# A fused attention and ternary feed-forward kernel: GpSimd adds twelve of the sixteen key chunks in every block, and the work around the row maxima is put in another order

## What is computed

```python
q = (x @ Wq.T + bq).reshape(Bx, Lx, H, hd)      # k_ and v the same way
scores = jnp.einsum('bqhd,bkhd->bhqk', q, k_) * scale + bias[None, None, None, :]
attn = jax.nn.softmax(scores, axis=-1)
ctx = jnp.einsum('bhqk,bkhd->bqhd', attn, v).reshape(Bx, Lx, Dx)
y = x + ctx @ Wo.T + bo                         # then layer norm with gamma, beta
x = _layernorm(x + attention)
x = _layernorm(x + ffn(x))                      # ffn: x @ Hadamard, 4 bit rounding, ternary weights
```

## Time and profile before

| what | value |
|---|---|
| median of 3 runs | 4854.95 us (4854.8 to 4855.31) |
| the profiled execution | 4854.98 us, its span 4853.2 us |
| TensorE busy | 4667.6 us, 96% |
| VectorE busy | 3318.9 us, 68% |
| ScalarE busy | 2596.1 us, 53% |
| GpSimd busy | 3642.9 us, 75% |

### The profile page before, as it was taken

How to read it: one execution, slowest core, us unless ns; L and a number is a source line. 1 busy time by engine, 2 the same in 40 slices (tenths; PEclk the granted TensorE clock), 3 DMA queues, 4 the chain that set the end, 5 groups by cost and what they waited for, 6 DMA issues and landing times.

```text
span 4853.2 us, 83960 instructions
## 1 busy us (share of the span) xinstructions
PE 4667.6 (96%) x24152; PEld 2375.4 (49%) x24152; DVE 3318.9 (68%) x5886; ACT 2596.1 (53%) x4891; POOL 3642.9 (75%) x1215
## 2 busy tenths in 40 slices
PE   7999999999899999999989999999999999999987
PEld 4445545554544555554454454555545444554434
DVE  3776676666777666666767767666676776667637
ACT  1455555554555555555455555555545655555545
POOL 1687777887488887777748877788875888877885
PEclk8899999999999999999999999999999999999998
DMA  9113232324411333322441223333334123332112
GB/s 207 32 40 71 58 72 63 70 66 105 127 40 43 66 70 69 75 62 64 114 112 41 56 60 71 67 66 67 76 112 99 50 48 66 70 68 59 29 53 72
DMA packets 245915, 346.30 MB, mean 71 GB/s; under 512 B 14801, under 2 KB 100561, under 8 KB 245458
## 3 DMA queue, kind: packets, MB, share of 16 engines
q1 hardware_dynamic: 245458, 340.73, 29.6%
HBM read 205.33 MB, written 33.55 MB: 49 GB/s over the span
## 4 chain that ended last, share of the span: by engine, by line
PE 78%; POOL 7%; DMA 6%; issue 4%; DVE 2%; ACT 1%; SPq 1%; POOLq 0%; ACTq 0%; DVEq 0%
PE ps_m L544 25%; PE ps_s L559 19%; PE ps_o L585 15%; PE ps_z L564 5%; DMA qst<-lo 5%; PE ps_z L531 4%; PE ps_m L505 3%; PE ps_z L499 3%; POOL acc L1117 3%; POOL prob L1143 1%; POOL prob L1147 1%; PE ps_s L505 1%; POOL prob L1132 1%; PE ps_s L499 1%; POOL prob L1126 1%
## 5 line engine op out<-in xcount | busy, mean ns | idle before, releaser
L926 DVE TENSOR_REDUCE umax<-ps_m 128x1 f32<-128x512 f32 x4096 | 2497.1, 681 | 757.7 <-PE ps_m L544 757.7
L1117 POOL TENSOR_TENSOR acc<-acc,prob 128x2048 f32<-128x2048 f32 x624 | 2858.2, 4580 | 151.2 <-ACT prob L783 101.7
L783 ACT ACTIVATE prob<-ps_s 128x512 f32<-128x512 f32 x4096 | 2131.5, 609 | 940.9 <-PE ps_s L559 927.1
L544 PE MATMUL ps_m<-kst,qst 97*128 97x512 f32 x4096 | 1872.0, 460 | 57.6 <-DMA qst<-lo 36.9
L559 PE MATMUL ps_s<-qst,kst 99*128 99x512 f32 x4096 | 1635.5, 400 | 12.2 <-ACT prob L783 9.9
L544 PEld LDWEIGHTS ps_m<-kst,qst 97*128 97x128 f32 x4096 | 777.7, 190 | 996.0 <-DVE umax L926 738.0
L585 PE MATMUL ps_o<-prob,vst 128*32 128x512 f32 x8192 | 976.7, 600 | 0.0
L559 PEld LDWEIGHTS ps_s<-qst,kst 99*128 99x128 f32 x4096 | 780.2, 191 | 138.9 <-ACT prob L783 31.5
L1117 POOL TENSOR_TENSOR acc<-prob 128x2048 f32<-128x2048 f32 x64 | 291.1, 4548 | 401.2 <-ACT prob L783 401.2
L585 PEld LDWEIGHTS ps_o<-prob,vst 128*32 128x32 f32 x8192 | 228.0, 110 | 530.8 <-issue 331.1
L1101 POOL TENSOR_TENSOR obuf<-obuf,zinv 128x512 f32<-128x512 f32 x64 | 82.4, 1287 | 442.1 <-ACT obuf L810 442.1
(11 more groups left out here) (114 smaller groups left out, 2528.8 us busy)
## 6 DMA issues: line engine op xcount, KB each, us to landing
xk<-in_xT_dram SPq DMA_DIRECT2D x66, 1024.0 KB, 8.6
xq<-in_xT_dram SPq DMA_DIRECT2D x65, 1024.0 KB, 5.8
kst<-hi SPq DMA_DIRECT2D x128, 256.0 KB, 6.8
qst<-hi SPq DMA_DIRECT2D x128, 256.0 KB, 5.2
wq<-in_wT_dram SPq DMA_DIRECT2D x65, 256.0 KB, 6.1
kst<-lo SPq DMA_DIRECT2D x64, 256.0 KB, 5.6
qst<-lo SPq DMA_DIRECT2D x64, 256.0 KB, 3.9
ctxT_dram<-obuf SPq DMA_DIRECT2D x64, 256.0 KB, 2.4
```

Source lines behind the costliest of these rows:

```text
L544: nc.tensor.matmul(ps_m[:, u % NMB, :], qst[k % 2][0:RSTACK, h, qt * P:(qt + 1) * P], kst[k // NQB % 2][0:RSTACK, h, kb * QB:(kb + 1) * QB ...
L783: nc.scalar.activation(prob[:, c % NPB, h, :], ps_s[:, (i * HG * NKC + HG * c + h) % NSB, :], ACT.Exp, scale=SCALE).then_inc(ex, 1)
L926: nc.vector.tensor_reduce(umax[:, m, kb:kb + 1], ps_m[:, u % NMB, :], AX.X, ALU.max).then_inc(mred, 1)
L1117: nc.gpsimd.tensor_tensor(acc[:], a, prob[:, c % NPB], ALU.add).then_inc(padd, 1)
```

## The change

1. `pe_sums` is `[12, 13, 14, 15]` in all blocks, so GpSimd makes eleven additions in every block, in the 16 early ones instead of ten.
2. The order within a pair's feed is the string `FEED`: the last three scores come ahead of the last three units.
3. The transpose of the maxima stands ahead of the sum of chunk 15.
4. The transfer of the maxima's row is issued by ScalarE, right behind its `mrow`, after a wait for it. SP issues the low part of the queries right behind the high parts.
5. `next_stage` (loads of inputs and weights for the next head group's projection) is issued by SP in block 0 of a batch and no longer at the end of the token stage.
6. At the program's start the second head group's projection is mixed with the 64 units of the first block.

```diff
+FEED = "msmsmsmsmssmsmsm"
 def pe_sums(i):
-    return [12, 13, 14, 15] if i >= NQB else [9, 12, 13, 14, 15]
+    return [12, 13, 14, 15]
...
@@ feed @@
-                for c in (2 * p, 2 * p + 1):
-                    for h in range(HG):
-                        u = HG * c + h
+                k, u = UP * p, UP * p
+                for what in FEED:
+                    if what == "s":
+                        c, h = divmod(k, HG)
+                        score(n, i, c, h, head=i == 0 and c == 0)
+                        k += 1
+                    else:
...
                             unit(u, n + 1, i + 1, (n >> 2) + 1 if i % NQB == NQB - 1 else None)
-                        score(n, i, c, h, head=i == 0 and c == 0)
+                        u += 1
@@ attend @@
                 for c in pe_sums(i):
+                    if c == NKC - 1 and not (last and i == NBLK - 1):
+                        maxima_to_rows(n + 1)
                     if c >= LATE_SUMS:
                         chunk_sums(n, i, c)
-                if not (last and i == NBLK - 1):
-                    maxima_to_rows(n + 1)
@@ SP, each block @@
+                        if i == 0:
+                            next_stage((n >> 2) + 1, (n >> 4) & (NB - 1), 1)
...
                             queries(n + 2, i + 2)
-                        if not (last and i == NBLK - 1):
-                            maxima(n + 1, i + 1)
-                        if not (last and i >= NBLK - 2):
                             low_queries(n + 2, i + 2)
@@ ScalarE @@
-            def maxima_rows(f):
+            def maxima_rows(f, k):
                 act.wait_ge(mtr, f + 1)
                 nc.scalar.activation(mrow[:], ps_m[0:2 * HG * NQB, 1, 0:P], ACT.Copy).then_inc(mcp, 1)
+                both = qst[k % 2][RM0:RM0 + 2].rearrange("p h (q x) -> p (h q) x", x=P)
+                act.wait_ge(mcp, f + 1)
+                act.dma_start(both.bitcast(F32), mrow[:].bitcast(F32)).then_inc(q_cur, 16)
@@ TensorE, start of the program @@
+            for t in range(NQB):
+                if t > 0:
+                    pe.wait_ge(k_lo, NQB + t)
+                keys_of(1, t, ps_z[:, :])
+                for u in range(UNITS // NQB * t, UNITS // NQB * t + UNITS // NQB // 2):
+                    unit(u, 0, 0, 0)
+                if t > 0:
+                    pe.wait_ge(v_cp, NQB + t)
+                values_of(t, ps_o[:, :])
+                for u in range(UNITS // NQB * t + UNITS // NQB // 2, UNITS // NQB * (t + 1)):
+                    unit(u, 0, 0, 0)
+                if t == 1:
+                    queries(1, ps_s[:, 0, :])
```

More of the change, by code:

```diff
@@ L326, in keys @@
                     keys_quarter(stage, b, s, t)
-                next_stage(stage, b, s)
             def next_stage(stage, b, s):
@@ L350, in next_queries @@
                 load_w(wq[:], 0, (k + 1) // NQB % NG).then_inc(wq_ld, 16)
[L352 to L356, removed]
             def store_context(n, i, stage):
@@ L420, in tokens @@
                             keys_quarter(bb * NG + NG + 1, bb, NG + 1, s - KEY_STEP - 1)
-                if not last:
-                    next_stage(b * NG + NG + 1, b, NG + 1)
             sp.dma_start(rows[0:1, 8:10, :], band.rearrange("a (b n) -> a b n", b=2)).then_inc(band_ld, 16)
@@ L437, in _ @@
             keys(0, 0, 0)
+            next_stage(0, 0, 0)
             sp.wait_ge(stk_ones, 4)
@@ L446, in _ @@
             next_queries(0, 0)
-            keys(1, 0, 1)
-            queries(1, 1)
-            low_queries(1, 1)
+            for t in range(NQB):
+                keys_quarter(1, 0, 1, t)
+                if t == 1:
+                    queries(1, 1)
+                    low_queries(1, 1)
             next_queries(0, 1)
-            maxima(0, 0)
             def batch(b, last):
@@ L718, in _ @@
             queries(0, ps_m[:, 0, :])
-            keys(1, 1)
-            queries(1, ps_m[:, 0, :])
             ternary()
@@ L724, in _ @@
             pe.wait_ge(tern_c, 5)
+            pe.wait_ge(q_lo, 1)
+            pe.wait_ge(wkv_ld, 64)
+            for t in range(NQB):
+                if t > 0:
[8 more added lines that the diff above has]
+                    unit(u, 0, 0, 0)
+                if t == 1:
+                    queries(1, ps_s[:, 0, :])
+            pe.wait_ge(k_lo, 2 * NQB)
+            pe.wait_ge(v_cp, 2 * NQB)
+            maxima_to_rows(0, first=True)
             pe.wait_ge(q_lo, 2)
-            for u in range(UNITS):
-                unit(u, 0, 0, 0)
-            maxima_to_rows(0, first=True)
             def batch(b, last):
@@ L755, in values_of, with keys @@
                                      bank, ACT.Copy).then_inc(v_cp, 1)
-            def keys(stage, s, q=None):
+            def keys(stage, s, kbank, vbank, q=None):
                 for t in range(NQB):
@@ L762, in keys @@
                         act.wait_ge(k_stk[t % 2], stage * (2 * NSTK) + NSTK)
-                    keys_of(stage, s, t, ps_m[:, 0, :])
-                    values_of(stage, s, t, ps_m[:, 1, :])
+                    if t == 2 and q is not None:
+                        act.wait_ge(q_stk, (q + 1) * NSTK)
+                    keys_of(stage, s, t, kbank)
+                    values_of(stage, s, t, vbank)
+                    if t == 1 and q is not None:
+                        act.wait_ge(k_stk[0], stage * (2 * NSTK) + NSTK)
+                        queries(q, q, ps_s[:, 0, :])
             def queries(f, k, bank):
@@ L806, in attend @@
                 if not (last and i == NBLK - 1):
-                    maxima_rows(n + 1)
+                    maxima_rows(n + 1, i + 1)
                 act.wait_ge(pv, n * NKC + 2 * NKC)
@@ L864, in _ @@
             act.wait_ge(bias_ld, 16)
-            keys(0, 0)
+            keys(0, 0, ps_m[:, 0, :], ps_m[:, 1, :])
             act.wait_ge(k_stk[0], 2 * NSTK)
             queries(0, 0, ps_m[:, 0, :])
[L868 to L871, removed]
+            keys(1, 1, ps_z[:, :], ps_o[:, :], 1)
+            maxima_rows(0, 0)
             def batch(b, last):
@@ L916, in quarter, with first_quarter, maxima @@
                 low_part(lo[:, 1], hi[:, 1], 1, i // NQB + 1, ps_z[:, :]).then_inc(k_lo, 1)
-            def maxima(f, i=None, last=False):
+            def first_quarter(t):
+                if t == 0:
+                    dve.wait_ge(q_stk, NSTK)
+                dve.wait_ge(k_hi, NQB + t + 1)
+                if t == 2:
+                    dve.wait_ge(q_stk, 2 * NSTK)
+                if t >= 2:
+                    dve.wait_ge(k_stk[t % 2], 2 * NSTK + NSTK)
+                low_part(lo[:, t % 2], hi[:, t % 2], 1, 1, ps_z[:, :]).then_inc(k_lo, 1)
+            def maxima(f, i=None, last=False, first=False):
                 for u in range(UNITS):
+                    if first and u % (UNITS // NQB) == UNITS // NQB // 2:
+                        first_quarter(u // (UNITS // NQB))
+                    if first and u == UNITS // 2 + NMB:
+                        queries(1, 1, ps_s[:, 0, :])
                     if i is not None and u == 2 * UP and not (last and i >= NBLK - 2):
@@ L1072, in _ @@
             queries(0, 0)
-            keys(1, 1, 1)
-            queries(1, 1)
             dve.wait_ge(tern_t, 1)
@@ L1078, in _ @@
             nc.vector.tensor_copy(wscale[:], ps_o[:]).then_inc(tern_c, 1)
-            maxima(0)
+            maxima(0, first=True)
             def batch(b, last):
```

## The result

The changed kernel takes 4829.89 us (4828.12 to 4830.85), the kernel before 4855.13 beside it: a ratio of 0.9944 [0.9927, 0.9961], faster by 0.6%. I had forecast 4876, slower, and the range began at 4835.

A forecast was written before the change was run, and what follows sets the result against it. TensorE's own order was taken as the bound, with GpSimd 1 to 2 us behind; 4854.98 + 79 (early blocks) - 25 (queries' low part) - 31 (feed) - 2 (start) = 4876 us, slower, range 4835 to 4912.

The forecast's parts named there:

- the feed's term: Pair feeds: the new order ends each 0.09 us earlier, eight feeds a block, in 44 late blocks: -31 us.
- ScalarE's pace takes the place of VectorE's: Feed: scores wait for exponentials instead of units for VectorE, so a feed gains 0.09 us, not 0.36.
- Eight take 4.11 ... they come every 0.50: Feed: eight exponentials take 4.11 us at 0.60 each, so they come every 0.50; exponential 4 ends at 177.26.
- The early blocks: 16 early blocks: GpSimd's added addition makes TensorE wait, period 63.8 against 58.89: +79 us.
- The mean of three tails, 6.62: Early blocks, behind the sum of `acc`: tail taken as 6.62 us, mean of 6.94, 7.10 and 5.81.
- The rival with the clock up: Early blocks: clock stays at 2.4 GHz after the waits, +45 instead of +79, 4842 us; chance 0.12.
- The low part of the queries: Block starts: SP issues it some 3 us earlier, so 41 blocks gain 0.6 each: -25 us.
- The start: Program start, projection mixed with units: first transpose near 135 against 141.57; -2 us taken, bounds -7 and +21.
- the lean toward the half clock: Program start: -6 was moved to -2 us, since halves at clock 0.50 cost up to 28 more (+21).
- The transpose's place and `next_stage`: Transpose one sum earlier, and block 0 loads needed over 200 us later: each forecast to change nothing.
- The sign: Whole kernel: slower, chance 0.56, against 0.25 for faster and 0.19 for same.
- the case in which the feed gets all of its 0.3 back: Rival, feed: whole wait regained, 0.3 a feed, -88 us, total 4819, faster; chance 0.13.

The follow-up runs named there:

- The filler: The changed kernel with three more matmuls, results unused, on TensorE ahead of its wait for the sum of `acc`, in early blocks only: 4806.74 us, 0.9899.
- the runs with the contexts first: Context of pairs 6 and 7 ahead of the wait for `acc`: on the change 5041.52 us; with chunk 9 also on TensorE in all blocks without a projection, 4990.82.

## Why the prediction was wrong

**The failed step is the size of the feed's term**, "0.09 earlier", eight times, 44 blocks, -31 us. The 44 late blocks became 87.4 shorter. With the feed of before in the change they are 60.6 longer, so the feed has some 60 of it, twice the forecast, and all else 26.8, where 25 were forecast; the feed alone on the kernel before gives 52 there. In batches 1 to 3 the mechanism was as said (ScalarE's pace takes the place of VectorE's; shorter exponentials shorten the feed, and the forecast of 3.9 from m0 to m7 held), in the last batch it was not (there shorter exponentials change nothing), and the number was read from rows that could not give it:

- "Eight take 4.11 ... they come every 0.50" took a stretch in which ScalarE was not the limit. In the order before, s6 and s7 reached it late (s7 at 177.74), so the stretch contains TensorE's lateness. With no late score it is 4.03, and (4.03 - 0.60)/7 = 0.49. Four exponentials of 0.01 less are 0.04, and 0.09 + 0.04 is the 0.13 to 0.14 that a pair shows in batches 1 to 3 (6.19 to 6.05).
- One feed of the first batch stood for all. In the last batch ScalarE starts its exponentials 0.14 sooner behind m0, so s7's limit is gone, and a pair gains 0.24 (6.19 to 5.95): 1.9 a block in its eight late blocks. That was in the trace of before: 4222.06 against 4221.30, 0.76, where the feed that I had read shows 174.66 - 173.73 = 0.93.
- The last batch's blocks 12 to 15 had no term. Blocks 12 to 14 gave 5.4, and only 0.5 of it up to the sum of `acc`, for which they wait for GpSimd as before. The rest is in the tails, 6.95, 7.10 and 5.81 before and 6.10, 4.43 and 4.43 after, the two short ones with the clock at 1.00.

By pairs: 36 x 8 x 0.14 + 8 x 8 x 0.24 = 56; pairs 0 and 1 give 0.2 each in batches 1 to 3, and so a little more. The trace of the change splits the late blocks without a token stage in another way: up to the sum of `acc` they are 1.18 shorter in batches 1 to 3 and 1.88 in the last, 54 in 41 blocks, and behind it, where the wait for `qst<-lo` was, 0.77 and 0.67, together 31. The three with a token stage give 2.5.

**The early blocks**: +79 forecast, +71.1 measured. In batches 1 to 3 the blocks behind a batch's first take 62.9 to 64.4, 63.7 in the mean (63.8 forecast), with tails of 5.88 to 7.37 and the clock at 0.50, in the short ones for the first 3 us. The mean of three tails, 6.62, stood for tails of that spread; that it hit their mean, 6.69, is in part luck. (63.8 - 58.89 is 4.9, not 4.95; times 16 it comes to 79 all the same.) The last batch is again the exception: its wait is split in two, the clock is up in the tail, and its four blocks cost 12.3 instead of the 19 to 20 of the others. The rival with the clock up is true of those four and of no others. The filler shows that the clock, and not something else behind the wait, makes the tail long.

The Trainium skill's figure for this addition ("GPSIMD Engine Reference", 3.1 Elementwise — side-by-side cycle accounting), 4497 ns, stands against 4578 ns in the mean of 640 additions after, and a spacing of 27.92/6 = 4.65 in a late block; the spacing of the trace was the better base.

**The low part of the queries**: right, -25 forecast. Alone, on the kernel before, it gives 35 over all blocks, 0.6 to 0.7 each, and in the change the 16 early ones spend theirs in the wait for GpSimd. In the groups by line, units' matmuls wait 2.5 us in all for `qst<-lo` where they waited 36.9, and scores wait 2.0 for `qst<-mrow`, as before, so nothing late shows behind ScalarE's issue.

```profile
L537 PE MATMUL ps_m<-kst,qst 97*128 97x512 f32 x4096 | 1714.9, 419 | 26.6 <-issue 16.4 <-DVE umax L957 3.7 <-DMA qst<-lo 2.5
```

**The start**: -2 forecast, -5.6 in the trace and -4.8 by undoing it. My working gave -6; the lean toward the half clock was unfounded (the granted clock is 0.90 from 70 to 105 us and 0.88 from 105 to 136). The transpose stands at 135.97, the working said 135. **The transpose's place and `next_stage`**: no stage shows a difference that would need them (in late blocks the change without its feed gives 26.8, the low part alone 26); they were not tried apart.

**The sign.** The terms are +79 and -58; the sum of +21 hangs on their difference. The misses are -31 (late blocks: 87.4 against 56), -5 (blocks 12 to 14), -8 (early) and -4 (start), all the same way: together -48, of which +1 at the end comes back. The range was too narrow below for that: it left out the case in which the feed gets all of its 0.3 back, and the last batch came near it (0.24). The late blocks did not start to wait: GpSimd ends at 518.03 in the block shown by the next rows, and TensorE comes to `acc` at 519.18.

```profile
490.11 27.92 POOL L1146 TENSOR_TENSOR acc<-acc,prob 128x2048 f32<-128x2048 f32 x6 [0.63 <-ACT prob L801]
```

**The change is two changes with opposite signs**: without the twelfth chunk it is worth 121 us, and the twelfth chunk takes 96 of them.

## What to carry to other kernels

To read an engine's pace from a group of instructions, first see that nothing in the group came late; the group's length is otherwise its supplier's. Where a small saving is multiplied by hundreds, read it in each batch or phase, since 0.05 a time was 15 us here and a second regime in the last batch decided as much. And before moving work out from between two steps, ask which *other* engine it was covering: the contexts looked like free filler for the wait, and were the cover of VectorE's reciprocal.

## What the runs showed of the hardware

- Not each idle time of TensorE was followed by half clock. Behind 3.9 to 4.4 us ahead of the sum of `acc` the clock was 0.50, and the tail took 5.73 to 7.37; in a tail of 5.88 it was 0.50 from 391.60 to 394.50 and 1.00 from 394.60 to 397.40. Behind 2.35, and behind 1.15 with work of 2.84 ahead of it, it was 1.00 and the tail took 4.43. Yet 2.01 in the last batch and 2.50 in the runs with the contexts first did drop it (0.58 and 0.50). One length did both: 2.65 was followed by 0.50 in the kernel before (tail 5.81) and by 1.00 in the same block of the run with twelve chunks alone (tail 4.43). What else tells these apart stays open.
- A stretch at half clock costs nothing where the engine would have waited anyway: 4.20 instead of 2.78 for the chunk sums in the last batch's early blocks was all inside GpSimd's time.
- Exponentials of 128x512 take 0.60 each and still follow one another every 0.49. With 448 columns eight take 3.72 to 3.75.
- In the last batch ScalarE's first exponential of a feed starts 0.14 to 0.17 sooner behind the first unit than in the others, before and after. The batches 1 to 3 run in a loop and the last is written out; I take the waits' computed values in the loop for the cause, but that was not tried.
